# One fused attention-and-norm kernel: queries and keys projected transposed for two tiles at a time, and their 96-row stacks built by DMA through a DRAM scratch

## The chip, the cores and the metric

One core of one Trainium2 chip. The metric is the device time of one execution in microseconds (us); shorter is better.

## The reference, cut to what matters

```python
# x is (4, 1024, 256); 16 heads of 16; one tile of the kernel is 128 tokens
h = _layernorm(x) * (1 + ca) + sa            # sa, ca, ga, sb, cb, gb from silu(c) @ wmod, per batch
q, k, v = split(h @ qkv_w + qkv_b)
scores = q k^T / sqrt(16); scores = where((dist > 0) & (dist <= 128) & (k_gpos >= 0), scores, NEG)
local = softmax(scores) @ v                  # a window of 128 keys before each query
rq, (rk, rv) = h @ rq_w + rq_b, mean_of_16(h) @ rkv_w + rkv_b      # 64 pooled tokens, 4 heads
remote = (masked softmax(rq rk^T) @ rv) @ rout_w + rout_b
gate = sigmoid(local @ gl_w + remote @ gr_w)
x = x + ga * ((gate * local + (1 - gate) * remote) @ out_w + out_b)
h = _layernorm(x) * (1 + cb) + sb
x = x + gb * FFN(h)
return x
```

The kernel computes the last block as `x1 + gb * (layernorm(h) * ln_g + ln_b)` (`add_u`, `scale3`, `finish`).

## The kernel before, in words

The 4096 tokens are 32 tiles of 128; a batch has 8 of them. The five engines run one software pipeline written out by hand: in slot t each engine walks its own fixed list, and the letters say which tile each stage of the list works on. A (tile t+2): layer norm, transpose, modulation (`hT`) and the projection `project_qk`. K (tile t+1): values, the latent branch, and the stacks of queries and keys. S (tile t): window scores for the row maxima. T (tile t-1): transposed scores with exponents (`scores_t`, `exps`), masks (`mask`) and the product with the values (`sum_v`). C (tile t-2): gate, mix and output projection. D (tile t-3): second norm and last block. A loop of 8 slots is unrolled and run 4 times. Nothing but these lists and semaphores sets the order: every engine executes in order, so one waiting instruction holds back all behind it.

To keep float32 accuracy with bfloat16 matmuls, q and k are each split into three bfloat16 terms, and six products of them are summed by stacking: a head's 16 columns stand six times, in 96 rows. `project_qk` writes q and k of one tile (128 tokens by 512 columns) to `p_qkv`; `copy_qk` on DVE adds the bias into `qkf`; `part1` and `part2` on ACT write the first and second term, in all the places in which they stand, into `qtok` and `ktok`; `res1` and `part3` on POOL make the remainders and the third term. `stack(t, u)` on PE then transposes 8 heads at a time (u = 0 to 3: queries, keys, queries, keys) into `p_x`, and `stack_copy` on ACT copies them to `qst` (queries) and `kst` (keys).

The score matmuls of `scores` read the stacks for the row maxima (`maxima` on DVE writes `mtok`). `max_t` transposes the maxima, `copy_shift` and `shift` on DVE write them under the queries as 16 more rows, of which `kst` selects one per head (`pick`, a row pattern written once at the start), so that `scores_t` computes score minus maximum, and `exps` on ACT follows. POOL zeroes what lies outside of the window (`mask(m, g)`, four groups of four heads), and `sum_v(m, g)` on PE waits for `masked[g]`. On ACT `gate_tanh(c)` stands between `exps(m, 4)` and `exps(m, 5)` and waits for POOL's `difference(c)`, which waits for DVE's `local_out(c)`. SP only stores finished tiles inside the loop. At the start SP loads the inputs, sends the rows that DVE's `modulation_rows` makes through DRAM (`mod_rows`) to all partitions, and then queues the load of the last 24 tiles of x.

## Time and profile before

| | |
|---|---|
| median of 3 runs | 657.01 us (656.66 to 661.27) |
| the profiled execution | 658.29 us, its span 656.5 us |
| mean granted TensorE clock | 0.974 |
| PE busy | 566.5 us (86%) |
| DVE busy | 503.8 us (77%) |
| ACT busy | 484.9 us (74%) |
| POOL busy | 417.7 us (64%) |
| moved by DMA | 17.48 MB, mean 27 GB/s |

The span runs from the first to the last instruction; the device time holds 1.8 us more. PE's busy time counts matmuls that overlap, so the distance between the starts of two neighbours says more than their durations. The DMA engines are idle after the first 60 us but for one store per tile.

### The profile page before, as it was taken

To read this page: it belongs to the slowest core of one execution; us is meant where nothing else is said; L and a number is where in the kernel's file an instruction comes from. 1 tells how busy PE (TensorE), PEld (TensorE's weight loads), DVE (VectorE), ACT (ScalarE), POOL (GpSimd) and SP (SyncE) were. 2 spreads that over 40 slices of the span, in tenths; PEclk is the share of its full clock that TensorE was granted. 3 is DMA by queue.
4 is the path that set the end of the run, shared out by engine and by line. 5 is a ranking of instruction groups with operands and counts; after the bars stand their busy time and mean duration, and the time that the engine had idled before them with its cause. 6 is when DMAs were issued, how large, how long until landed. Compare 5 with 4: busy or idle time off the path is not lost. (4 is left out here: it accounts for less than half of the span.)

```text
span 656.5 us, 22130 instructions
## 1 busy us (share of the span) xinstructions
PE 566.5 (86%) x7535; PEld 415.4 (63%) x7535; DVE 503.8 (77%) x1390; ACT 484.9 (74%) x1066; POOL 417.7 (64%) x616
## 2 busy tenths in 40 slices
PE   2739999999979999999979999999979999999972
PEld 2237666776657666667756666766756666666651
DVE  5637888888868787888868788888868888888864
ACT  1687787778868787777768788777767778877760
POOL 3335566667756577766657576776656576677673
PEclk9879999999999999999989999999989999999986
DMA  8183000000000000000000000000000000000000
GB/s 262 63 292 96 2 2 2 11 10 10 11 15 9 10 10 7 6 10 10 10 15 10 9 10 11 10 2 10 10 15 10 9 10 11 10 6 6 11 18 16
DMA packets 13761, 17.48 MB, mean 27 GB/s; under 512 B 2980, under 2 KB 11836, under 8 KB 13628
## 3 DMA queue, kind: packets, MB, share of 16 engines
q1 hardware_dynamic: 10764, 14.52, 6.4%
q10 hardware_dynamic: 2864, 1.31, 0.8%
q8 instruction: 68, 1.11, 0.7%
q14 instruction: 65, 0.53, 0.3%
HBM read 11.61 MB, written 4.22 MB: 24 GB/s over the span
## 5 line engine op out<-in xcount | busy, mean ns | idle before, releaser
L554 ACT ACTIVATE pr<-p_y 128x512 f32<-128x512 f32 x232 | 135.0, 597 | 30.4 <-PE p_y L802 26.6
L1171 DVE TENSOR_REDUCE mtok<-p_x 128x3 bf16<-128x480 f32 (+3 forms) x192 | 113.5, 591 | 53.3 <-issue 29.6
L399 POOL TENSOR_SCALAR_AFFINE_SELECT pr<-pr 128x512 f32<-128x512 f32 x132 | 88.5, 670 | 49.7 <-ACT pr L554 46.0
L801 PE MATMUL p_y<-qst,kst 112*128 112x128 bf16 x464 | 71.3, 220 | 27.5 <-ACT pr L554 26.7
L403 POOL TENSOR_SCALAR_AFFINE_SELECT pr<-pr 128x512 f32<-128x512 f32 x116 | 89.7, 773 | 0.0
L802 PE MATMUL p_y<-qst,kst 112*128 112x128 bf16 x528 | 77.9, 219 | 3.1 <-ACT pr L556 3.1
L409 POOL TENSOR_TENSOR rstd<-ve,half 128x1 f32<-128x1 f32 x104 | 63.7, 620 | 26.5 <-DVE ve L1094 24.7
L427 POOL TENSOR_TENSOR dif<-local,rem 128x272 f32<-128x272 f32 x34 | 25.9, 762 | 85.0 <-DVE local L1224 85.0
L705 PE MATMUL p_qkv<-wqk,hT 128*128 128x512 f32 x136 | 69.1, 632 | 2.1 <-issue 1.2
L801 PEld LDWEIGHTS p_y<-qst,kst 112*128 112x128 bf16 x464 | 45.2, 101 | 40.4 <-issue 30.5
L545 ACT ACTIVATE qst<-p_x 96x1024 bf16<-96x1024 bf16 x66 | 67.3, 1019 | 2.5 <-PE p_x L748 0.5
L816 PE MATMUL p_pv<-pr,vp 128*18 128x128 f32 x1984 | 67.5, 275 | 1.2 <-POOL pr L403 1.2
L545 ACT ACTIVATE kst<-p_x 96x1024 bf16<-96x1024 bf16 x66 | 67.3, 1019 | 0.0
L778 PE MATMUL p_x<-kst,qst 96*32 96x160 bf16 x1792 | 61.9, 236 | 0.0
L816 PEld LDWEIGHTS p_pv<-pr,vp 128*18 128x18 f32 x1984 | 48.8, 98 | 18.1 <-issue 16.6
L594 ACT ACTIVATE th<-dif 128x16 f32<-128x16 f32 x34 | 7.8, 229 | 70.7 <-POOL dif L427 70.7
L802 PEld LDWEIGHTS p_y<-qst,kst 112*128 112x128 bf16 x528 | 50.1, 98 | 13.7 <-issue 4.2
L383 POOL TENSOR_TENSOR res<-qkf,qtok 128x256 f32<-128x256 f32 x34 | 23.3, 685 | 55.8 <-ACT ktok L532 55.8
L778 PEld LDWEIGHTS p_x<-kst,qst 96*32 96x32 bf16 x1792 | 28.1, 95 | 22.5 <-issue 10.3
L748 PE MATMUL p_x<-ident_bf,qtok 128*96 128x128 bf16 x528 | 40.3, 219 | 2.2 <-POOL ktok L391 1.4
L715 PE MATMUL p_qkv<-wv,hT 128*128 128x272 f32 x132 | 41.4, 439 | 0.0
L748 PE MATMUL p_x<-ident_bf,ktok 128*96 128x128 bf16 x528 | 40.3, 219 | 0.3 <-ACT kst L545 0.3
(159 smaller groups left out, 1498.6 us busy)
## 6 DMA issues: line engine op xcount, KB each, us to landing
out_y<-y SPq DMA_DIRECT2D x32, 128.0 KB, 2.4
x_all<-in_x SPq DMA_DIRECT2D x1, 3072.0 KB, 17.9
pr<-in_wmod SPq DMA_DIRECT2D x1, 1024.0 KB, 10.1
row<-in_rows SPq DMA_DIRECT2D x1, 816.0 KB, 7.0
x_all<-in_x SPq DMA_DIRECT2D x1, 768.0 KB, 4.9
wqk<-in_qkv_w ACTq DMA_DIRECT2D x1, 512.0 KB, 3.8
pr<-in_wmod SPq DMA_DIRECT2D x1, 512.0 KB, 5.3
pr<-mod_rows SPq DMA_DIRECT2D x1, 512.0 KB, 4.0
```

The source lines that it names most:

```text
L399: ins = pool.affine_select(out=own, in_=own, compare_op=ALU.is_ge, fill=0.0, base=-1, pattern=[[0, 4], [1, P]], channel_multiplier=-1)
L403: ins = pool.affine_select(out=prev, in_=prev, compare_op=ALU.is_ge, fill=0.0, base=-1, pattern=[[0, 4], [-P, P]], channel_multiplier=P + 1)
L409: pool.tensor_tensor(rstd_[:, :], ve_[:, :], half[:, :], ALU.pow).then_inc(s_rstd, 1)
L545: act.activation(dst, p_x[u % 2][0:KS, :].bitcast(BF16).rearrange("p (h n) -> p h n", h=8), ACT.Copy)\
L554: act.activation(pr[:, 2 * i:2 * i + 2, :, :], src, ACT.Exp).then_inc(exp_done[i], 1)
L705: ins = pe.matmul(p_qkv[:, :], hT[:, t[1] % 2, k, :], wqk[:, k, :], start=(k == 0), stop=(k == KC - 1))
L748: ins = pe.transpose(dst[:, j * P:(j + 1) * P], src[:, 8 * (u // 2) + j, :], ident_bf[:, :])
L778: ins = pe.matmul(win[g * QG:(g + 1) * QG, h - h0, :], qst[0:KS, t[1] % RING, h, g * QG:(g + 1) * QG], keys[:, at:at + WIN], start=False, ...
L801: pe.matmul(p_y[i % 2][:, at:at + P], kst[0:KS + H, h, (n - 1) % NB, :], q, start=True, stop=True)
L802: ins = pe.matmul(p_y[i % 2][:, at + P:at + 2 * P], kst[0:KS + H, h, n % NB, :], q, start=True, stop=True)
L816: ins = pe.matmul(p_pv[32 * j:32 * j + VC, g * P:(g + 1) * P], vp[:, (n - 1 + a) % RING, h, :], pr[:, h, a, :], start=(a == 0 or n % NB == ...
L1171: dve.tensor_reduce(mtok[:, KS + h0:KS + h1], p_x[i % 2][:, 0:(h1 - h0) * w].rearrange("p (h n) -> p h n", n=w), AX_X, ALU.max, negate=Tru ...
```

## The change

Queries and keys are projected transposed: `project_half` computes, for a pair of tiles (256 tokens as the moving columns), the queries in one slot and the keys in the next, so that features lie on the partitions. The pipeline is longer: A works on tile t+4, the projection (P) on t+3, the split into terms (Q) on t+2. The three terms are written once each into `terms`. `stack`, `stack_copy`, `qtok`, `ktok` and `pick` are gone. Instead SP stores the three terms of a half to a DRAM scratch (`store_terms`, 128 partitions by 6 runs of 512 bytes) and reads the stack back with six transfers (`load_stack`, each 16 partitions by 16 runs of 512 bytes). Queries are handled in even slots, keys in odd ones. The shift is one row under the queries, moved by SP from `mrow` (`shift`), with a constant row of ones under the keys. The edge mask of a score group is written by four matmuls on column quarters instead of one. The start of the program runs four shortened slots.

```diff
--- before.py
+++ after.py
-Q_SLOTS = {1: (2, 5, 1), 2: (1, 6, 4), 3: (0, 1, 1)}
-K_SLOTS = {1: (0, 3, 1), 2: (3, 6, 2), 3: (4, 5, 1)}
-
+Q_TERMS = (0, 0, 0, 1, 1, 2)
+K_TERMS = (0, 1, 2, 0, 1, 0)
...
+            def shift(t):
+
+                wait_apart(sp, (mrow_ready, done(t)), (st_psum[NP - 1], done(back(t, 4))))
+                sp.dma_start(q_of(t)[KS:KS + 1, :, :], mrow[:, :]).then_inc(shift_loaded[t[1] % 2], 16)
+
+            def store_terms(r):
+
+                half = r[1] % 2
+                wait_apart(sp, (part3_ready, done(r)), (stack_loaded[half], halves(back(r, 2), 16 * NTERM)))
+                sp.dma_start(scr[half].rearrange("t p n -> p t n"), terms[:, half, :, :, :].rearrange("p s b n -> p (s b) n"))\
+                  .then_inc(terms_stored[half], 16)
+
+            def load_stack(r):
+
+                half = r[1] % 2
+                pair = pair_of(r)
+                wait_apart(sp, (terms_stored[half], halves(r, 16)), (st_psum[NP - 1], done(back(r, 7 if half else 3))))
+                n = pair[1] % NB
+                for i in range(NTERM):
+                    if half:
+                        dst = kst[i * HD:(i + 1) * HD, :, n:n + 2, :].rearrange("d h r n -> d h (r n)")
+                    else:
+                        dst = qst[i * HD:(i + 1) * HD, n // 2 % 2, :, :]
+                    s0 = (K_TERMS if half else Q_TERMS)[i] * KC
+                    sp.dma_start(dst, scr[half][s0:s0 + KC].rearrange("b (h d) n -> d (b h) n", d=HD))\
+                      .then_inc(stack_loaded[half], 16)
...
+            def slot(t, stages):
+                r, m, d = back(t, -2), back(t, 1), back(t, 3)
+                Q, T, D_ = ("Q" in stages, "T" in stages, "D" in stages)
+                if T:
+                    shift(m)
+                if Q:
+                    store_terms(r)
+                if Q and t[1] % 2:
+                    load_stack(r)
+                if D_:
+                    store(d)
+                if Q and t[1] % 2 == 0:
+                    load_stack(r)
+
+            slot((0, -2), "Q")
+            slot((0, -1), "Q")
...
             def res1(t):
 
                 pool.wait_ge(part1_ready, done(t))
-                pool.tensor_tensor(heads(res[:, 0:D]), heads(qkf[:, 0:D]), slots(qtok, Q_SLOTS[1])[:, :, 0, :], ALU.subtract)
-                pool.tensor_tensor(heads(res[:, D:2 * D]), heads(qkf[:, D:2 * D]), slots(ktok, K_SLOTS[1])[:, :, 0, :],
-                                   ALU.subtract).then_inc(res_ready, 1)
+                half = t[1] % 2
+                pool.tensor_tensor(qkf[:, half, :, :], qkf[:, half, :, :], terms[:, half, 0, :, :], ALU.subtract)\
+                    .then_inc(res_ready, 1)
 
             def part3(t):
+
                 pool.wait_ge(part2_ready, done(t))
-                pool.tensor_tensor(slots(qtok, Q_SLOTS[3])[:, :, 0, :], heads(res[:, 0:D]),
-                                   slots(qtok, Q_SLOTS[2])[:, :, 0, :], ALU.subtract)
-                pool.tensor_tensor(slots(ktok, K_SLOTS[3])[:, :, 0, :], heads(res[:, D:2 * D]),
-                                   slots(ktok, K_SLOTS[2])[:, :, 0, :], ALU.subtract).then_inc(part3_ready, 1)
+                half = t[1] % 2
+                pool.tensor_tensor(terms[:, half, 2, :, :], qkf[:, half, :, :], terms[:, half, 1, :, :], ALU.subtract)\
+                    .then_inc(part3_ready, 1)
...
             def part1(t):
 
+                half = t[1] % 2
                 act.wait_ge(qk_copied, done(t))
-                act.wait_ge(stack_psum[3], done(back(t, 1)))
-                act.activation(slots(qtok, Q_SLOTS[1]), rep(qkf[:, 0:D], Q_SLOTS[1]), ACT.Copy)
-                act.activation(slots(ktok, K_SLOTS[1]), rep(qkf[:, D:2 * D], K_SLOTS[1]), ACT.Copy).then_inc(part1_ready, 1)
+                act.wait_ge(terms_stored[half], halves(back(t, 2), 16))
+                act.activation(terms[:, half, 0, :, :], qkf[:, half, :, :], ACT.Copy).then_inc(part1_ready, 1)
 
             def part2(t):
+
+                half = t[1] % 2
                 act.wait_ge(res_ready, done(t))
-                act.activation(slots(qtok, Q_SLOTS[2]), rep(res[:, 0:D], Q_SLOTS[2]), ACT.Copy)
-                act.activation(slots(ktok, K_SLOTS[2]), rep(res[:, D:2 * D], K_SLOTS[2]), ACT.Copy).then_inc(part2_ready, 1)
-
-            def stack_copy(t, u):
-
-                act.wait_ge(stack_psum[u], done(t))
-                act.wait_ge(st_psum[NP - 1], done(back(t, 3)))
-                hs = slice(8 * (u // 2), 8 * (u // 2) + 8)
-                dst = kst[0:KS, hs, t[1] % NB, :] if u % 2 else qst[0:KS, t[1] % RING, hs, :]
-                act.activation(dst, p_x[u % 2][0:KS, :].bitcast(BF16).rearrange("p (h n) -> p h n", h=8), ACT.Copy)\
-                   .then_inc(stack_copied[u], 1)
+                act.activation(terms[:, half, 1, :, :], qkf[:, half, :, :], ACT.Copy).then_inc(part2_ready, 1)
...
-                a, k, m, c = back(t, -2), back(t, -1), back(t, 1), back(t, 2)
-                A, K, S, T, C = ("A" in stages, "K" in stages, "S" in stages, "T" in stages, "C" in stages)
+                a, r, m, c = back(t, -LEAD), back(t, -2), back(t, 1), back(t, 2)
+                A, Q, S, T, C = ("A" in stages, "Q" in stages, "S" in stages, "T" in stages, "C" in stages)
+                if Q:
+                    part1(r)
                 if C:
                     out_t(c)
                 if T:
                     lat_oT(m)
-                if K:
-                    part2(k)
-                if T:
                     exps(m, 0)
+                if Q:
+                    part2(r)
+                if T:
                     exps(m, 1)
                 if S:
                     lat_exp(t)
...
                     exps(m, 5)
                     remote(m)
                     exps(m, 6)
-                if K:
-                    stack_copy(k, 0)
-                    stack_copy(k, 1)
-                if T:
                     exps(m, 7)
+                if S:
+                    lat_pT(t)
                 if C:
                     mixed_t(c)
-                if K:
-                    stack_copy(k, 2)
-                if A:
-                    part1(a)
-                if S:
-                    lat_pT(t)
-                if K:
-                    stack_copy(k, 3)
 
...
-            def project_qk(t):
-                pe.wait_ge(hT_ready, done(t))
-
-                pe.wait_ge(rem_ready, done(back(t, 3)))
-                if t[1] < 2 and isinstance(t[0], int):
-                    pe.wait_ge(v_copied, done(back(t, 1)))
-                for k in range(KC):
-                    ins = pe.matmul(p_qkv[:, :], hT[:, t[1] % 2, k, :], wqk[:, k, :], start=(k == 0), stop=(k == KC - 1))
+            def project_half(t):
+
+                pair, half = pair_of(t), t[1] % 2
+                pe.wait_ge(hT_ready, done(back(pair, -1)))
+
+                pe.wait_ge(rem_ready, done(back(t, 4)))
+                pe.wait_ge(v_copied, done(back(t, 2)))
+                pe.wait_ge(qk_copied, done(back(t, 1)))
+                r = pair[1] % 4
+                for b in range(KC):
+                    for k in range(KC):
+                        ins = pe.matmul(p_qkv[:, 2 * b * P:2 * (b + 1) * P], wqk[:, k, half * D + b * P:half * D + (b + 1) * P],
+                                        hT[:, r:r + 2, k, :], start=(k == 0), stop=(k == KC - 1))
                 ins.then_inc(qk_psum, 1)
...
-            def stack(t, u):
...
-                src = (qtok, ktok)[u % 2]
-                dst = p_x[u % 2][0:KS, :].bitcast(BF16)
-                for j in range(8):
-                    ins = pe.transpose(dst[:, j * P:(j + 1) * P], src[:, 8 * (u // 2) + j, :], ident_bf[:, :])
-                ins.then_inc(stack_psum[u], 1)
...
-                if i == 0:
-                    pe.wait_ge(stack_copied[0], done(t))
-                    pe.wait_ge(stack_copied[1], done(t))
-                    pe.wait_ge(stack_copied[2], done(t))
-                elif i == 1:
-                    pe.wait_ge(stack_copied[3], done(t))
-                else:
-                    pe.wait_ge(s_max[i - 2], done(t))
+                if i == 0 and t[1] % 2 == 0:
+                    for half in range(2):
+                        pe.wait_ge(stack_loaded[half], halves(back(t, -half), 16 * NTERM))
+                pe.wait_ge(s_max[(i - 2) % NS], done(t if i >= 2 else back(t, 1)))
...
-                    pe.matmul(ends, ident_bf[:, :], edge[:, :].unsqueeze(1).to_broadcast([P, h1 - h0, 2 * QG]).rearrange("p h (e n) -> p h e n", n=QG),
-                              start=True, stop=True)
+                    for g in range(4):
+                        pe.matmul(ends[g * QG:(g + 1) * QG], ident_bf[:, g * QG:(g + 1) * QG],
+                                  edge[:, :].unsqueeze(1).to_broadcast([P, h1 - h0, 2 * QG]).rearrange("p h (e n) -> p h e n", n=QG),
+                                  start=True, stop=True, tile_position=(0, g * QG))
...
-                pe.transpose(p_qkv[:, 0:P // 2].bitcast(BF16), mtok[:, :], ident_bf[:, :]).then_inc(mT_psum, 1)
+                pe.transpose(p_qkv[0:H, 0:P // 2].bitcast(BF16), mtok[:, :], ident_bf[:, :]).then_inc(mT_psum, 1)
...
-                pe.wait_ge(shift_ready, done(t))
+                pe.wait_ge(shift_loaded[t[1] % 2], halves(t, 16))
...
-                if K:
-                    stack(k, 0)
                 if T:
                     scores_t(m, 7)
-                if K:
-                    stack(k, 1)
-                if A:
-                    project_qk(a)
+                if PR:
+                    project_half(h)
                 if C:
                     mixed_t(c)
-                if K:
-                    stack(k, 2)
                 if S:
                     lat_p_t(t)
-                if K:
-                    stack(k, 3)
                 if C:
                     project_out(c)
...
             def copy_qk(t):
 
+                half = t[1] % 2
                 dve.wait_ge(qk_psum, done(t))
-                dve.wait_ge(part3_ready, done(back(t, 1)))
-                dve.tensor_tensor(qkf[:, :], p_qkv[:, :], row[:, R_QK:R_QK + 2 * D], ALU.add).then_inc(qk_copied, 1)
+                dve.wait_ge(part3_ready, done(back(t, 2)))
+                dve.tensor_tensor(qkf[:, half, :, :], p_qkv[:, :].rearrange("p (b n) -> p b n", b=KC),
+                                  bc(bqk[:, half, :], 2 * P), ALU.add).then_inc(qk_copied, 1)
...
             def copy_shift(t):
+
                 dve.wait_ge(mT_psum, done(t))
-                dve.tensor_copy(mrow[KS:KS + H, :], p_qkv[KS:KS + H, 0:P // 2].bitcast(BF16)).then_inc(mrow_ready, 1)
-
-            def shift(t):
-
-                dve.wait_ge(mrow_ready, done(t))
-                dve.tensor_copy(qst[KS:KS + H, t[1] % RING, :, :],
-                                mrow[KS:KS + H, :].unsqueeze(1).to_broadcast([H, H, P])).then_inc(shift_ready, 1)
+                dve.wait_ge(shift_loaded[(t[1] - 1) % 2], halves(back(t, 1), 16))
+                dve.tensor_copy(mrow[:, :], p_qkv[0:H, 0:P // 2].bitcast(BF16)).then_inc(mrow_ready, 1)
...
             dve.wait_ge(loaded_x0, 16)
-            b0, b1 = (0, 0), (0, 1)
-            bn1(b0)
-            moments1(b0)
-            add_eps1(b0)
-            norm1(b0)
+            dve.wait_ge(su_act, SA_QK)
+            slot((0, -4), "A")
+            slot((0, -3), "AP")
             weights()
-            copy_qk(b0)
-            bn1(b1)
-            moments1(b1)
-            add_eps1(b1)
-            copy_v(b0)
-            norm1(b1)
-            pool_tokens(b0)
-            pool_twice(b0)
+            dve.wait_ge(loaded_x1, 16)
+            slot((0, -2), "APQ")
             modulation_rows()
-            copy_qk(b1)
             dve.wait_ge(loaded_bd, 16)
-            copy_rk(b0)
-            copy_rq(b0)
-            copy_rv(b0)
-            spread_rv(b0)
+            slot((0, -1), "APQK")
...
```

On POOL, in a slot of the loop (mask 0 is the pair of AFFINE_SELECT, `xb` is `add_bias`, `dif` is `difference`), before:

```order
L290 ISA
L399 AFFINE_SELECT pr<-pr 128x4x128
L403 AFFINE_SELECT pr<-pr 128x4x128
L389 TENSOR_TENSOR qtok<-res,qtok 128x16x16
L391 TENSOR_TENSOR ktok<-res,ktok 128x16x16
L423 REGISTER_ALU
L427 TENSOR_TENSOR dif<-local,rem 128x272
```

and now:

```order
L458 TENSOR_TENSOR rstd<-ve,half 128x1
L440 TENSOR_TENSOR terms<-qkf,terms 128x512
L291 ISA
L448 AFFINE_SELECT pr<-pr 128x4x128
L452 AFFINE_SELECT pr<-pr 128x4x128
L485 ISA
L485 TENSOR_TENSOR xb<-x_all,obg 128x256
L472 REGISTER_ALU
L476 TENSOR_TENSOR dif<-local,rem 128x272
```

The third term (`part3`) has moved from behind mask 0 to ahead of it, as one instruction of 512 elements, and `add_bias` from the slot's start to behind mask 0.

On PE, the last third of a slot (L705 is `project_qk`, L748 `stack`, L872 `mixed_t`, L836 `lat_p_t`, L880 `project_out`, L816 `sum_v` of groups 1 to 3), before:

```order
L748 MATMUL p_x<-ident_bf,ktok 96x128 x8
L705 MATMUL p_qkv<-wqk,hT 128x512 x2
L872 MATMUL p_misc<-cst,mix 128x128 x2
L748 MATMUL p_x<-ident_bf,qtok 96x128 x8
L836 MATMUL p_a<-cst,lp 128x128 x2
L748 MATMUL p_x<-ident_bf,ktok 96x128 x8
L880 ISA
L880 MATMUL p_misc<-wo,mixT 128x256
L880 ISA
L880 MATMUL p_misc<-wo,mixT 128x256
L816 MATMUL p_pv<-pr,vp 18x128 x24
```

and now:

```order
L723 MATMUL p_qkv<-hT,wqk 128x256 x4
L871 MATMUL p_misc<-cst,mix 128x128 x2
L835 MATMUL p_a<-cst,lp 128x128 x2
L879 ISA
L879 MATMUL p_misc<-wo,mixT 128x256
L879 ISA
L879 MATMUL p_misc<-wo,mixT 128x256
L814 MATMUL p_pv<-pr,vp 18x128 x24
```

`mixed_t`, `lat_p_t` and `project_out` now follow each other with nothing between them.

On SP, the loop's beginning, before:

```order
L349 UNCONDITIONAL_BRANCH
L349 ISA
L343 ISA
L343 DMA out_y<-y 128x256
L342 REGISTER_ALU
```

and now (slots 0 and the beginning of slot 1):

```order
L397 UNCONDITIONAL_BRANCH
L397 ISA
L350 DMA qst<-mrow 1x16x128
L291 ISA
L356 DMA scr_q<-terms 128x6x256
L291 ISA
L376 ISA
L376 DMA out_y<-y 128x256
L291 ISA
L371 DMA qst<-scr_q 16x16x256 x6
L291 ISA
L350 DMA qst<-mrow 1x16x128
```

In an even slot the six loads of the query stack stand behind the store of y and ahead of the next slot's shift row. (In an odd slot the key loads stand ahead of the store of y.)

## Rows read from the trace of the kernel before

**Rows 1.** Waits of PE over the whole execution: us in total, times, longest us.

```profile
PE p_y L801 <- ACT pr L554: 26.7, 30, 1.0
```

**Rows 2.** PE's timeline over one slot: start us, us busy; idle time in brackets.

```profile
299.50 0.23 PE L790 MATMUL p_qkv<-ident_bf,mtok 128*128 128x128 bf16 x1
...
302.56 0.22 PE L801 MATMUL p_y<-qst,kst 112*128 112x128 bf16 x1
...
306.24 0.63 PE L816 MATMUL p_pv<-pr,vp 128*18 128x128 f32 x16
306.81 0.23 PE L772 MATMUL p_x<-edge,ident_bf 128*128 128x128 bf16 x1
...
311.13 0.22 PE L801 MATMUL p_y<-qst,kst 112*128 112x128 bf16 x1 [0.88 <-ACT pr L554]
...
311.35 0.61 PE L748 MATMUL p_x<-ident_bf,ktok 128*96 128x128 bf16 x8
311.80 1.94 PE L705 MATMUL p_qkv<-wqk,hT 128*128 128x512 f32 x4
313.57 0.38 PE L872 MATMUL p_misc<-cst,mix 128*128 128x128 f32 x2
...
314.91 1.08 PE L880 MATMUL p_misc<-wo,mixT 128*128 x4
315.92 1.51 PE L816 MATMUL p_pv<-pr,vp 128*18 128x128 f32 x48
317.36 0.23 PE L790 MATMUL p_qkv<-ident_bf,mtok 128*128 128x128 bf16 x1
```

**Rows 3.** ACT's timeline over the same slot.

```profile
302.98 1.33 ACT L554 ACTIVATE pr<-p_y 128x512 f32<-128x512 f32 x2 [0.43 <-PE p_y L802]
...
310.41 0.58 ACT L554 ACTIVATE pr<-p_y 128x512 f32<-128x512 f32 x1
...
316.83 0.36 ACT L576 ACTIVATE lpT<-p_a 128x256 f32<-128x256 f32 x1
```

**Rows 4.** POOL's timeline over the same slot.

```profile
305.04 0.64 POOL L403 TENSOR_SCALAR_AFFINE_SELECT pr<-pr 128x512 f32<-128x512 f32 x1
...
309.48 0.77 POOL L427 TENSOR_TENSOR dif<-local,rem 128x272 f32<-128x272 f32 x1 [2.50 <-DVE local L1224]
```

**Rows 5.** POOL's groups by form: busy us, mean ns of one, idle before.

```profile
L280 POOL TENSOR_TENSOR wo<-rem,pr 128x512 f32<-128x512 f32 x2 | 2.5, 1265 | 0.0
```

**Rows 6.** DVE's timeline over the same slot.

```profile
299.80 0.23 DVE L1176 COPY mrow<-p_qkv 16x128 bf16<-16x128 bf16 x1
...
314.38 0.72 DVE L1272 SCALAR_TENSOR_TENSOR y<-h,rstd,ux 128x256 f32<-128x256 f32 x1
```

**Rows 7.** DMA view: a queue (packets, MB, share), then issues (KB, us to landing).

```profile
q10 hardware_dynamic: 2864, 1.31, 0.8%
...
x_all<-in_x SPq DMA_DIRECT2D x1, 3072.0 KB, 17.9
...
b<-mod_rows SPq DMA_DIRECT2D x1, 512.0 KB, 8.5
```

**Rows 8.** SP's timeline at the start of the program.

```profile
32.44 0.32 SPq L332 DMA_DIRECT2D mod_rows<-qst  x1
34.56 0.35 SPq L334 DMA_DIRECT2D pr<-mod_rows  x1
...
37.17 0.59 SPq L336 DMA_DIRECT2D b<-mod_rows  x1
37.81 0.45 SPq L338 DMA_DIRECT2D x_all<-in_x  x1
```

**Rows 9.** All engines' timeline at the start of the program.

```profile
17.05 3.75 PE L705 MATMUL p_qkv<-wqk,hT 128*128 128x512 f32 x4 [1.16 <-issue]
...
27.20 0.73 DVE L1052 TENSOR_SCALAR qst<-p_y 4x256 f32<-4x256 f32 x2
...
47.07 0.29 PE L790 MATMUL p_qkv<-ident_bf,mtok 128*128 128x128 bf16 x1 [9.36 <-ACT kst L516]
```

More of the change, by code:

```diff
@@ L69, with build @@
 R_END = R_GR + HD
-def build(nc, x, qkv_w, rq_w, rq_b, rkv_w, rk_b, rout_w, rout_b, out_w, c_t, wmod, rows, consts, out):
+def build(nc, x, qk_b, ones, qkv_w, rq_w, rq_b, rkv_w, rk_b, rout_w, rout_b, out_w, c_t, wmod, rows, consts, out):
     ctx = ExitStack()
@@ L461, in slot @@
                     mask(m, 1)
-                    mask(m, 2)
                 if D:
@@ L1412, in constants @@
         c[LD + q, C_IND + q * CH:C_IND + (q + 1) * CH] = 1
-    for h in range(H):
-        c[KS + h, C_SEL + h] = 1
     c[CH:, C_VAL] = 1
```

222 lines of the change are left out of this document (100 added, 122 removed).

## The prediction

> **What bounds the kernel now.** I read PE's timeline first. A slot runs from one `max_t` (L790) to the next, 299.50 to 317.36, 17.86 us [rows 2], and the starts stand close behind each other: PE works nearly all the time. What ends its few waits is told by its list of waits: `scores_t` waits for exponents in 30 of the slots, 26.7 us together [rows 1]; the row at 311.13 is one such place [rows 2]. The reader is to see why it waits there, since this is a chain through all engines that removing PE work doesn't shorten. I count T from the slot's start, 299.50. `scores(t, 5)` begins at T 7.31 (306.81); DVE then takes its maxima, scales the second norm and makes `local`; POOL subtracts at T 9.98 (309.48) [rows 4], 2.67 behind; ACT's tanh lets `exps(m, 5)` start at T 10.91 [rows 3], and the last `scores_t` starts at T 11.63 [rows 2]. From `scores(t, 5)` to there are 4.32 us, whatever PE does meanwhile. So PE work bounds most of the slot and this chain one part of it, and a cut of PE work counts only where no such chain takes over.
>
> **Part 1, what PE loses.** Four groups of stack transposes go: one takes 0.45 from start to start (311.35 to 311.80) [rows 2], together 1.8 us a slot. One stands just ahead of the wait at 311.13, so without it that wait grows by the same 0.45. The projection keeps its 1.77 us (311.80 to 313.57) [rows 2]: eight passes of 256 columns for four of 512. An edge matmul takes 0.16 with its weights (306.81; the wider ones somewhat more); in four quarters it costs between 0.1 and 0.3. I take 0.1, as the score matmuls in quarters also overlap, and so 0.06 gained six times. If all of this arrived, a slot would take 17.86 - 1.8 - 0.36 = 15.7 us.
>
> **Part 2, what ACT and DVE lose.** Stack copies and the spreading of terms leave ACT, and the shift copy leaves DVE. Neither bounds a slot (74% and 77% busy), so I give them nothing but shorter queues.
>
> **Part 3, the third term moves ahead of mask 0.** This is the term that I trust most. Before, mask 0 was done at T 6.18 (305.04 + 0.64) [rows 4] and `sum_v(m, 0)` began at T 6.74 [rows 2], without a wait. Now ACT runs `exps(m, 0)` at T 3.48 [rows 3], then `part2` to about T 4.7, and POOL must do `part3` before mask 0. As one POOL instruction on 512 elements it has a near row: 1.265 us [rows 5]. It ends at T 6.0, mask 0 is a pair of 0.6 and 0.64 and ends at T 7.3, and `sum_v(m, 0)`, which PE would now reach at T 6.5, starts there. `scores(t, 5)` follows 0.57 behind as before, at T 7.9, and with the unchanged 4.32 the last `scores_t` starts at T 12.2 instead of 11.63.
>
> **Part 4, the tail of the slot.** From there 0.22 + 1.77 + 0.22 bring PE to `lat_p_t` at T 14.4. ACT now copies `lpT` ahead of `mixT`: two copies of 256 columns, 0.36 each [rows 3]. The transposes take 0.38 to be there [rows 2], so `mixT` is there at about T 15.5 and `project_out` starts at T 15.6, against T 15.41 before; two stacks used to fill this time. Then 1.01 for `project_out` (314.91 to 315.92) and 1.44 for `sum_v` (to 317.36) [rows 2]: the slot ends at T 18.1. So all of PE's saving turns into waits, and a slot without any DMA trouble costs +0.2. Bounds: -0.5, if `part3` runs at twice that row's speed, to +0.6.
>
> **Part 5, the shift row.** `mrow` is there at T 0.53 (299.80 + 0.23) [rows 6]. The nearest row for a small transfer and its wait is that of the modulation rows: issued at 32.44, the next one at 34.56, 2.1 us [rows 8]. In an odd-to-even step SP is free, the row lands at T 2.8, and `scores_t(m, 0)` wanted it at T 3.06 (302.56) [rows 2]: no cost. In an even-to-odd step it is different. SP is in order, and ahead of the shift it waits for y, which is done at T 15.6 (314.38 + 0.72) [rows 6], then issues the store and six loads, each 0.4 to 0.5 us to issue [rows 8]. The shift's packets also stand behind those of the loads: 6 x 256 = 1536 runs of 512 bytes. No row shows such loads. Below is the mean packet of the ACT queue: 0.8% of 16 x 656.5 us over 2864 packets [rows 7] is 29 ns on one engine, 1.8 ns with 16, so the loads would be bound by their issue, 2.9 us. Above is the load of x: 3072 rows of 1 KB in 17.9 less 2.1 fixed, 5.1 ns a row, 7.9 us. Less what stood ahead of it (the last broadcast landed 8.5 behind 37.17, at 45.7, and x at 37.81 + 17.9 = 55.7 [rows 7, 8]) it is 3.3 ns, 5.0 us. I take this, as it is the same queue and direction, and a row of half the size is hardly half the price. Then the loads land at T 16.1 + 2.1 + 5.0 = 23.2, the shift just behind at T 5.3 of the odd slot, 2.3 us late (0.4 and 5.2 at the ends). Behind the waiting `scores_t` stands everything that PE has left in the slot, and ACT's `exps(m, 0)`, POOL's `part3` and mask 0 behind it: the slot grows by all of it.
>
> **Part 6, the keys in an odd slot.** `part3` ends at T 6.0 + 2.3 = 8.3. The store takes 2.1 + 768 x 3.3 ns = 4.6, the loads 7.1: T 20.1 with SP's own steps. The slot ends at T 20.4. Nothing is lost, but with a margin of a few tenths; at 5.1 ns the keys come 3.9 us late as well.
>
> **Part 7, the start.** PE began slot 0 at 47.07 [rows 9]. The new start hides less: DVE needs tile 0 and 1 through transposes and modulation and then a projection at the low clock (3.75 us against 1.94 in the loop; the clock was at 1.2 GHz there) [rows 2, 9] before it makes the weights, and the same again with tile 2 before `modulation_rows`, which stood at 27.20 [rows 9]. I put this at 11 us (5 to 14): two such waits of some 6 us. SP then issues the load of x at 48.8 instead of 37.81 and it lands 17.9 later, at 66.7 [rows 7, 8]. All transfers for the stacks are issued behind it on the same queue: query terms to 69.2, query loads to 76.3 with the key store behind them to 78.8, key loads 7.1 more, 86. That is +39 us (27 with the lower price and the smaller delay).
>
> **The sum.** 657.0 + 39 + 32 x 0.2 + 16 x 2.3 = 739; I say **740 us**, slower. The profiled execution was 658.29 with a span of 656.5, so the new one should show a span near 739. A change within 1% can't be told from none here.
>
> **A rule that speaks against the change.** The loads write 16 partitions each. If the rate depends on how many partitions a transfer spans, six of them in a row are slow one after the other. The Trainium skill, page "SBUF — State Buffer", section on the DMA port swizzle, says just this: four neighbouring partitions share a port, 16 ports at 27.2 GB/s. By that page 16 partitions reach four ports, and the six loads, 786 KB, would take about 7.2 us, an estimate; no row here shows a transfer on so few partitions. This is a rival.
>
> **Rivals.** (1) The loads are slow, 7.9 us by the undeducted x row: the shift is 5.2 late, the keys 3.9, 16 x 9.1 = 146 and the start 4 more: 845; with something between this and my price, 790. For it speaks the narrow destination, against it the 29 ns packets of the ACT queue. Chance 0.27. (2) The loads are cheap, 1.8 ns: 657 + 30 + 6 + 6 = 699, chance 0.18. (3) The other side: the chain of part 3 isn't there, because PE's list doesn't really wait for mask 0 (`part3` much shorter than the row of 512), and the shift comes in time. Slots of 15.7 give -2.16 x 32 = -69, the start +39: 627. It decides at 1.2 us a slot, since the start must be won back first. The idle 0.56 ahead of `sum_v` is all the room that the trace shows, so 0.05. (4) Long waits lower PE's clock again in the loop, as at the start: each low stretch doubles matmul time, and 760 to 800 comes out even with quick loads; 0.08. My own case, 720 to 760, has 0.42.
>
> **The range** takes in the cheap loads and most of the slow ones: 695 to 820. Slower by over 1%: 0.94; faster by over 1%: 0.05; within: 0.01.
>
> **What would show it.** Right: PE's `scores_t` of group 0 waits for a DMA in every second slot, some 2 us; `sum_v(m, 0)` waits for POOL in nearly all; `project_out` waits for ACT by 0.9; slots alternate, about 18 and 20 us; slot 0 begins at 80 to 90 us with SP's first store of terms behind x. Wrong: `scores(t, 0)` of even slots waiting for the key stack (rival 1); even slots under 17 us; the first stacks there before 60 us, if transfers of one queue overtake each other.

## The result

| | before | changed |
|---|---|---|
| median | 657.55 us (656.66 to 661.27) | 803.75 us (800.23 to 806.76) |
| profiled span | 656.5 us | 799.6 us |
| mean granted TensorE clock | 0.974 | 0.857 |

The ratio is 1.2208, with a 95% interval of 1.2142 to 1.2274. The changed kernel is 146 us slower. That lies in the range of 695 to 820, but outside my own likeliest case, 720 to 760, and 64 us above the forecast of 740.

### The profile page after: what moved, and what is told of

Read it like the earlier page. It is cut to its first block, busy times and chain, and to the rows that moved or that the text cites. A ratio compares the mean times of both kernels' runs of the same rounds, so it can differ in the third digit from the quotient of the medians.

```text
span 799.6 us, 21397 instructions
## 1 busy us (share of the span) xinstructions
PE 569.0 (71%) x7131; PEld 429.9 (54%) x7131; DVE 473.4 (59%) x1366; ACT 304.9 (38%) x864; POOL 385.9 (48%) x552
## 3 DMA queue, kind: packets, MB, share of 16 engines
q1 hardware_dynamic: 94110, 54.55, 36.4%
## 4 chain that ended last, share of the span: by engine, by line
issue 38%; PE 21%; POOL 21%; DVE 6%; DMA 6%; ACT 4%; SPq 2%; POOLq 1%; DVEq 0%; ACTq 0%
PE p_qkv L723 9%; PE p_misc L879 5%; POOL rstd L458 4%; POOL qkf L433 4%; POOL dif L476 3%; POOL xb L485 3%; POOL pr L452 2%; POOL pr L448 2%; DMA scr_q<-terms 2%; ACT pr L589 2%; POOL terms L440 2%; ACT mixT L634 2%; SPq L371 2%; DMA qst<-mrow 1%; PE p_misc L871 1%
## 5 line engine op out<-in xcount | busy, mean ns | idle before, releaser
L799 PE MATMUL p_y<-qst,kst 97*128 97x128 bf16 x464 | 80.1, 239 | 91.1 <-DMA qst<-mrow 53.3
L799 PEld LDWEIGHTS p_y<-qst,kst 97*128 97x128 bf16 x464 | 49.1, 109 | 113.4 <-DMA qst<-mrow 60.3
L440 POOL TENSOR_TENSOR terms<-qkf,terms 128x512 bf16<-128x512 f32 x34 | 39.3, 1157 | 136.2 <-ACT terms L581 136.2
L800 PE MATMUL p_y<-qst,kst 97*128 97x128 bf16 x528 | 89.7, 243 | 15.5 <-DMA qst<-mrow 13.0
L723 PE MATMUL p_qkv<-hT,wqk 128*128 128x256 f32 x280 | 85.1, 458 | 0.9 <-ACT hT L565 0.9
L814 PE MATMUL p_pv<-pr,vp 128*18 128x128 f32 x1984 | 69.5, 280 | 3.2 <-POOL pr L452 2.5
L800 PEld LDWEIGHTS p_y<-qst,kst 97*128 97x128 bf16 x528 | 55.4, 109 | 27.9 <-DMA qst<-mrow 14.3
L723 PEld LDWEIGHTS p_qkv<-hT,wqk 128*128 128x128 f32 x280 | 61.0, 229 | 11.4 <-ACT hT L565 1.3
L814 PEld LDWEIGHTS p_pv<-pr,vp 128*18 128x18 f32 x1984 | 49.1, 99 | 22.8 <-issue 14.6
L879 PE MATMUL p_misc<-wo,mixT 128*128 (+1 forms) x136 | 38.6, 407 | 29.0 <-ACT mixT L634 29.0
L597 ACT ACTIVATE oT<-p_pv 128x512 f32<-128x512 f32 x34 | 20.3, 597 | 74.3 <-PE p_pv L814 67.3
L769 PE MATMUL p_x<-edge,ident_bf 128*32 128x192 bf16 (+1 forms) x672 | 47.4, 264 | 0.0
L879 PEld LDWEIGHTS p_misc<-wo,mixT 128*128 128x128 f32 x136 | 23.5, 193 | 38.9 <-ACT mixT L634 27.4
L490 POOL TENSOR_TENSOR ux<-x,b 128x256 f32<-128x256 f32 x35 | 26.0, 742 | 37.4 <-DVE x L1230 24.6
```

Of the source, the lines that this page charges most:

```text
L440: pool.tensor_tensor(terms[:, half, 2, :, :], qkf[:, half, :, :], terms[:, half, 1, :, :], ALU.subtract)\
L723: ins = pe.matmul(p_qkv[:, 2 * b * P:2 * (b + 1) * P], wqk[:, k, half * D + b * P:half * D + (b + 1) * P], hT[:, r:r + 2, k, :], start=(k ...
L799: pe.matmul(p_y[i % 2][:, at:at + P], kst[0:KS + 1, h, (n - 1) % NB, :], q, start=True, stop=True)
L800: ins = pe.matmul(p_y[i % 2][:, at + P:at + 2 * P], kst[0:KS + 1, h, n % NB, :], q, start=True, stop=True)
L814: ins = pe.matmul(p_pv[32 * j:32 * j + VC, g * P:(g + 1) * P], vp[:, (n - 1 + a) % RING, h, :], pr[:, h, a, :], start=(a == 0 or n % NB == ...
L879: ins = pe.matmul(p_misc[:, 0:D], mixT[:, k * P:(k + 1) * P], wo[:, bass.ds(batch(t) * (KC * D // NB) + k * D, D)], start=(k == 0), stop=( ...
```

## The profile after

The page of the changed kernel: busy times, the granted clock, and the busiest DMA queue.

```profile
PE 569.0 (71%) x7131; PEld 429.9 (54%) x7131; DVE 473.4 (59%) x1366; ACT 304.9 (38%) x864; POOL 385.9 (48%) x552
...
PEclk9755799998988898989989688989889597979896
...
q1 hardware_dynamic: 94110, 54.55, 36.4%
```

PE issues fewer matmuls and is busy for as long as before: the stacks' work went, and a lower clock took its place. ACT fell from 74% to 38% busy, and none of that shows as a gain in the time.

The waits of PE (us in total, times, longest us); all are in the loop but the wait for `kst`, which is in the start:

```profile
PE p_y L799 <- DMA qst<-mrow: 53.3, 17, 5.5
PE p_y L799 <- ACT pr L589: 37.9, 30, 1.5
PE p_misc L879 <- ACT mixT L634: 29.0, 34, 1.0
PE p_x L761 <- DMA kst<-scr_k: 26.5, 1, 26.5
...
PE p_y L800 <- DMA qst<-mrow: 13.0, 3, 4.4
```

The wait for exponents was 26.7 [rows 1]. The waits for the shift row (53.3 + 13.0 = 66.3 us, since L799 and L800 are both `scores_t`) and for `mixT` are new. PE's timeline through an even slot (L788 is `max_t`, L799 `scores_t`, L814 `sum_v`, L769 an edge mask, L723 `project_half`, L879 `project_out`) and the odd slot behind it:

```profile
329.78 0.22 PE L788 MATMUL p_qkv<-ident_bf,mtok 128*16 128x128 bf16 x1
...
332.72 0.22 PE L799 MATMUL p_y<-qst,kst 97*128 97x128 bf16 x1
...
336.78 0.63 PE L814 MATMUL p_pv<-pr,vp 128*18 128x128 f32 x16
337.23 0.24 PE L769 MATMUL p_x<-edge,ident_bf 128*32 128x128 bf16 x4
...
341.44 0.22 PE L799 MATMUL p_y<-qst,kst 97*128 97x128 bf16 x1 [1.33 <-ACT pr L589]
...
341.68 1.96 PE L723 MATMUL p_qkv<-hT,wqk 128*128 128x256 f32 x8
...
344.92 1.10 PE L879 MATMUL p_misc<-wo,mixT 128*128 x4 [0.84 <-ACT mixT L634]
...
347.28 0.22 PE L788 MATMUL p_qkv<-ident_bf,mtok 128*16 128x128 bf16 x1
...
355.89 0.29 PE L799 MATMUL p_y<-qst,kst 97*128 97x128 bf16 x1 [5.51 <-DMA qst<-mrow]
...
362.36 0.94 PE L814 MATMUL p_pv<-pr,vp 128*18 128x128 f32 x16
...
373.17 0.22 PE L788 MATMUL p_qkv<-ident_bf,mtok 128*16 128x128 bf16 x1
```

The even slot takes 17.50 us, against 17.86 before [rows 2]. The odd one takes 25.89. It is among the three odd slots with the longest wait for the row, 5.1 to 5.5 us; eleven others wait 4.0 to 4.4, slot 3 waits 1.1 and slot 1 not at all. Its `scores_t` starts at T 8.61 instead of T 2.94, 5.67 later, and everything stands behind it. From there to `sum_v` it takes 6.47 instead of 4.06. The windows of just these two stretches, odd and even (us, busy times, then the granted clock, DMA share and GB/s), say why:

```profile
355.89:362.36 6.47, 6.47 (x69) 4.24 (x69) 2.73 (x6) 3.98 (x13) 3.03 (x4) 0.50 0.19 62
```

```profile
332.72:336.78 4.06, 3.83 (x69) 2.57 (x67) 3.16 (x8) 3.63 (x13) 2.44 (x4) 1.00 0.06 19
```

After the 5.51 us without a matmul, PE works at 0.50, the level of 1.2 GHz, for the same 69 matmuls. SP's timeline shows where the row stood: the load of the queries is issued at 346.02 and the row (L350) at 348.99, and it was used at 355.89.

```profile
346.02 2.78 SPq L371 DMA_DIRECT2D qst<-scr_q  x6
348.99 0.52 SPq L350 DMA_DIRECT2D qst<-mrow  x1
...
361.73 2.78 SPq L371 DMA_DIRECT2D kst<-scr_k  x6
```

The start, on the same engine: the long load of x, then the first store of terms, whose issue alone is held for 10.67 us, and the loads behind it.

```profile
48.04 0.45 SPq L344 DMA_DIRECT2D x_all<-in_x  x1
48.62 10.67 SPq L356 DMA_DIRECT2D scr_q<-terms  x1
66.42 2.78 SPq L371 DMA_DIRECT2D qst<-scr_q  x6
...
75.43 2.76 SPq L371 DMA_DIRECT2D kst<-scr_k  x6
```

**Where the time went**, from the starts of `max_t`. The table counts slot 0 as part of the start, since the changed kernel enters it and then waits in it for the keys until 83.19.

| | before | changed | difference |
|---|---|---|---|
| up to slot 1 | 66.99 | 104.02 | +37.0 |
| slots 1 to 31 | 560.7 | 666.4 | +105.8 |
| behind the last | 28.9 | 29.2 | +0.3 |

The 16 odd slots rose from 18.17 to 24.37 on average, +99. Of this, some 63 us are waits for the row, and 29 are the stretch from `scores_t` to `sum_v`, as run 3 shows. The 15 even ones cost 6 us more together: seven take 17.50, the others 18.3 to 20.3. Five of these (slots 8, 16, 18, 24 and 28) have the low clock in a part of the slot, three (2, 10 and 26) don't.

## The experiments

Medians; in brackets the kernel before on the same chip; "loop" is slots 1 to 31 in the profile (before: 560.7, changed: 666.4), read from one execution of each. The changed kernel itself was not timed again on these chips, so a run's ratio is to be held against its 1.2208.

**Run 1, the row on another queue.** Everything else as in the changed kernel.

```diff
-                if T:
-                    shift(m)            # SP
+                if T:
+                    shift(m)            # ACT, ahead of lat_oT, act.dma_start(...)
```

> The changed kernel, but the shift row is issued by ACT (between out_t and lat_oT), so it travels on ACT's DMA queue and not behind the six query loads on SP's. Theory Q (the row is late only because it stands behind the loads on one queue): the 17 long waits of scores_t for the row (53.3 us) fall under 1 us each, odd slots go from about 25 to about 18 us, and the loss in low clock behind the waits goes as well. The key stack, hidden so far in the long odd slots, then comes about 1 us late in even slots. Total 690 us (680 to 710). Rival E (the 16 DMA engines are simply busy with the loads, whatever the queue): the row stays 5 us late and the total stays within 10 us of 804.

776.98 us [659.99], 1.1768 (1.1717 to 1.1819), loop 642.3. SP's loads, ACT's issue of the row, and PE's `scores_t` behind it:

```profile
347.10 3.42 SPq L366 DMA_DIRECT2D qst<-scr_q  x6
349.44 0.51 ACTq L579 DMA_DIRECT2D qst<-mrow  x1
```

```profile
355.29 0.23 PE L798 MATMUL p_y<-qst,kst 97*128 97x128 bf16 x1 [3.32 <-DMA qst<-mrow]
```

Nothing stands ahead of the row on its own queue, and still PE has it only 5.85 us after its issue, 8.19 after that of the loads. I had expected 690 if order were all, and within 10 us of 804 if the loads held the row back on any queue. The result is nearer to the second: a queue of its own doesn't get the row past the loads' data. Whether the two share the DMA engines or the way into SBUF is not told apart.

**Run 2, the same bytes to spread partitions.** The copies of a head's 16 features are interleaved in the stack, so that a load still writes 16 partitions, but every sixth one and not neighbours. The products and their sum are the same.

```diff
-dst = kst[i * HD:(i + 1) * HD, :, n:n + 2, :]
+dst = kst[i:KS:NTERM, :, n:n + 2, :]
-dst = qst[i * HD:(i + 1) * HD, n // 2 % 2, :, :]
+dst = qst[i:KS:NTERM, n // 2 % 2, :, :]
```

> The changed kernel, but row i of a feature's six terms stands at partition 6d+i instead of 16i+d, for queries and keys alike: the same six loads of 256 runs of 512 bytes, each now spread over 96 partitions instead of 16 neighbouring ones. Theory N (the loads are slow because a transfer writes 16 neighbouring partitions): they become bound by their issue, 2.8 us, instead of the 7.6 us that the trace shows (first issue at 346.02, the row behind them there at 355.8, less 2.1 fixed). The row is then at most 1 us late, and the total is about 685 to 700 us. Rival P (the price is 4.9 ns for each run of 512 bytes, wherever it goes): nothing changes, 800 to 808.

759.23 us [659.99], 1.1499 (1.1445 to 1.1554), loop 629.0. The DMA view (count, KB, median us from issue to landing) of the changed kernel, then of this one:

```profile
qst<-scr_q SPq DMA_DIRECT2D x102, 128.0 KB, 4.5
```

```profile
qst<-scr_q SPq DMA_DIRECT2D x102, 128.0 KB, 2.7
```

The same 54.55 MB take 23.3% of the engines' time instead of 36.4%. So the neighbouring destinations were what made a run dear. The time stayed well above the 685 to 700 that I expected, because the row still stands behind six issues, and their issue is now longer (SP, and the `scores_t` that ends the wait):

```profile
333.04 3.87 SPq L371 DMA_DIRECT2D qst<-scr_q  x6
337.10 0.56 SPq L350 DMA_DIRECT2D qst<-mrow  x1
```

```profile
340.31 0.29 PE L799 MATMUL p_y<-qst,kst 97*128 97x128 bf16 x1 [2.90 <-DMA qst<-mrow]
```

**Run 3, PE kept busy through the wait.** 24 matmuls of 512 columns, added work whose result is overwritten, ahead of the wait in odd slots.

```diff
+                pe.wait_ge(exp_done[(i - 2) % NP], done(t if i >= 2 else back(t, 1)))
+                if i == 0 and t[1] % 2 == 0:
+                    for _ in range(24):
+                        pe.matmul(p_y[0][:, :], ident_bf[:, :], <smask0, 512 columns>, start=True, stop=True)
                 pe.wait_ge(shift_loaded[t[1] % 2], halves(t, 16))
-                pe.wait_ge(exp_done[(i - 2) % NP], done(t if i >= 2 else back(t, 1)))
```

> The changed kernel with extra work that the result doesn't need: in odd slots PE runs 24 bfloat16 matmuls of 512 columns, about 5.2 us, into p_y ahead of scores_t(m, 0), while the shift row is on its way. Theory C (after 5.5 us without work PE's clock stands at 1.2 GHz for some 7 us, and this costs 2.4 us in each odd slot on top of the wait): the granted clock goes back to about 0.95 and the total falls by 16 x 2.4 = 38, to 765. Rival (the 2.4 us are the chain through ACT and POOL, not the clock): the clock rises and the total stays at 804 or grows by a few us where the wait is shorter than the extra work.

792.63 us [659.99], 1.2006 (1.1971 to 1.2041), loop 655.4. The added matmuls, the first score matmul, and the windows of the stretches before and behind it:

```profile
357.04 5.34 PE L795 MATMUL p_y<-smask,ident_bf 128*128 128x512 bf16 x24
362.22 0.22 PE L803 MATMUL p_y<-qst,kst 97*128 97x128 bf16 x1
```

```profile
361.00:366.30 5.30, 5.06 (x78) 3.10 (x76) 2.65 (x6) 3.65 (x13) 2.46 (x4) 1.00 0.07 20
...
370.80:376.00 5.20, 4.31 (x17) 3.44 (x17) 3.27 (x12) 2.13 (x6) 3.70 (x6) 0.67 0.79 89
```

`scores_t` to `sum_v` takes 4.07 again (362.22 to 366.29), so the idle time does lower the clock and costs 2.4 us there. Summed over the 16 odd slots, this stretch gives back 28.8 us. But the 24 matmuls last 5.2 us: with them `scores_t` starts at T 8.12 in every odd slot, where it started at T 7.1 to 7.5 in eleven of them and at T 2.9 and 4.2 in slots 1 and 3. That costs 17.6 us. The difference is the 11 us by which the loop got shorter, where I had expected 38. In this slot the clock falls later as well, at 370.86, where PE had waited 1.24 us for exponents; that happens in some slots of the changed kernel too, and run 8 shows that it hangs on this wait.

**Run 4, `mixT` first.** `mixed_t` on ACT ahead of `lat_pT`.

```diff
+                if C:
+                    mixed_t(c)
                 if S:
                     lat_pT(t)
-                if C:
-                    mixed_t(c)
```

> The changed kernel, but ACT copies mixT ahead of lpT at the end of a slot. My step on the tail (project_out waits for mixT behind lpT, 0.84 to 1.0 us in each of 34 slots, 29.0 us in all, and this sets the slot's end): 804 - 33 x 0.8 = 777. Rival (mask 3 on POOL or the DVE's list sets the slot's end, so the wait only moves to sum_v): within 5 us of 804.

789.81 us [659.99], 1.1991 (1.1919 to 1.2064), loop 652.1. PE's wait for `mixT` falls from 0.84 to 0.35 in a slot, and a clean even slot (one without a low clock or a wait for the row) from 17.50 to 17.02. That is over half of the 0.8 that I had expected, and the median is 12.8 above the expected 777:

```profile
326.96 1.10 PE L879 MATMUL p_misc<-wo,mixT 128*128 x4 [0.35 <-ACT mixT L634]
```

**Run 5, x on ACT's queue.** The load of the last 24 tiles of x is issued by ACT behind its second short slot of the start.

```diff
-            sp.dma_start(x_all[:, (XPAD + NB) * D: ...], x[NB:NT] ...).then_inc(loaded_x, 16)
...
             slot((0, -3), "AP")
+            act.dma_start(x_all[:, (XPAD + NB) * D: ...], x[NB:NT] ...).then_inc(loaded_x, 16)
```

> The changed kernel, but the load of the last 24 tiles of x is issued on ACT's queue early in the start (after the second shortened slot), not on SP's queue ahead of the first store of terms. Theory S (the first stacks are late because their transfers stand behind 3 MB of x on one queue): that store, whose issue took 10.67 us from 48.62 and which was there at 66.4, is there at about 52 (the five broadcasts remain ahead), slot 0 scores start at 66 to 70 instead of 83.2, and the total falls by 14 to 17 us from about 806 on this chip, to 790. Rival (the late modulation rows, 42.75 against 32.44, and the six loads themselves set the start): within 5 us of 806.

796.10 us [658.83], 1.2069 (1.2003 to 1.2134). The start's wait for keys falls from 26.5 to 18.0 us, and slot 1 begins at 94.2 instead of 104.0: 10 us, where I had expected 14 to 17. The loop is at 668.7, about as it was.

```profile
PE p_x L761 <- DMA kst<-scr_k: 18.0, 1, 18.0
```

**Runs 6 to 8, edits together.** Run 6 is runs 1 and 2. Run 7 adds runs 4 and 5. Run 8 also puts ACT's `gate_tanh(c)` behind `exps(m, 5)`.

> Both of e1 and e2: the shift row on ACT's queue and the six terms of a feature spread over 96 partitions. Each alone left the row 2 to 4 us late, on its own queue because the 16 engines were still busy with the slow loads, with quick loads because it stood behind them on the queue. If these two are the whole of it, the row now costs at most 0.5 us, no slot sees the low clock, the keys land at T 14.5, and odd slots come down to the 17.5 us of even ones: 683 to 692. Rival: something else makes odd slots long (SP's order, the keys), and they stay above 19: over 705.

> e6 with the mixT copy ahead of the lpT copy on ACT (e4) and the x load on ACT's queue (e5). If the effects add: 687 less 15 (0.48 us a slot, as e4 measured) less 14 to 17, so 655 to 660, level with the kernel before. All four are repairs of the change's own costs.

> e7 with ACT's gate_tanh behind exps(m, 5) instead of ahead of it. The chain scores(t, 5), maxima, second norm, local, POOL difference, tanh, exps(m, 5), last scores_t made PE wait 1.33 us in each slot with the change (0.88 to 1.0 before). If this chain is what kept PE's saving from showing, the wait goes and slots fall by up to 1.3 us: 657 less up to 40, so 617 to 635. Rival: mask 3 on POOL, or the mix for mixed_t, is late instead and takes most of it: above 645.

| | median | ratio (95%) | loop |
|---|---|---|---|
| run 6 | 708.22 [658.83] | 1.0759 (1.0705 to 1.0813) | 573.8 |
| run 7 | 685.81 [658.83] | 1.0354 (1.0303 to 1.0405) | - |
| run 8 | 671.98 [658.83] | 1.0174 (1.0127 to 1.0220) | 549.6 |

The profiled execution of run 7 took 695.28 us, well above its median, so its loop is not compared. All three runs missed what I had expected of them, 683 to 692, 655 to 660 and 617 to 635.

Runs 1 and 2 alone gave 24 and 37 us in the loop, together 93: with both, the row lands 2.2 us after its issue (median) and the sum of its waits is 6.2 us. That run 6 is still 16 us above the range is for the greater part the clock at another place. In seven slots `project_half`, behind PE's wait for exponents, takes 3.3 to 3.7 us instead of 1.97, 10 us together, as here in slot 13:

```profile
330.83 0.22 PE L798 MATMUL p_y<-qst,kst 97*128 97x128 bf16 x1 [1.32 <-ACT pr L587]
...
331.22 3.41 PE L722 MATMUL p_qkv<-hT,wqk 128*128 128x256 f32 x8
```

The granted clock over 331.10 to 334.50 is 0.57. In run 8 the wait for exponents is gone, and `project_half` takes 1.97 in all 32 slots. So the low clock at this place came with that wait, though the same wait is not followed by it in most slots, and what decides that I can't say. Even slots of run 8 stay at 17.02. A new wait of 0.86 us stands ahead of `project_half`:

```profile
PE p_qkv L723 <- issue: 29.4, 32, 1.1
```

```profile
349.68 0.23 ACT L625 ACTIVATE th<-dif 128x16 f32<-128x16 f32 x1 [1.52 <-POOL dif L467]
349.81 0.38 ACT L618 ACTIVATE rem<-p_qkv 128x272 f32<-128x272 f32 x1
```

```profile
350.29 1.96 PE L723 MATMUL p_qkv<-hT,wqk 128*128 128x256 f32 x8 [0.86 <-issue]
```

The profile names "issue", but the code tells which wait it is: `project_half` writes the bank from which ACT's `remote` (L618) copies, and `remote` stood behind `gate_tanh` (L625) and its wait for POOL.

**Runs 9 to 11, on the kernel before.** Run 9 has the quarters of the edge masks alone, run 10 has `gate_tanh` behind `exps(m, 6)`, run 11 has both.

```diff
-                    pe.matmul(ends, ident_bf[:, :], <edge>, start=True, stop=True)
+                    for g in range(4):
+                        pe.matmul(ends[g * QG:(g + 1) * QG], ident_bf[:, g * QG:(g + 1) * QG], <edge>,
+                                  start=True, stop=True, tile_position=(0, g * QG))
```

```diff
-                if C:
-                    gate_tanh(c)
                 if T:
                     exps(m, 5)
                     remote(m)
                     exps(m, 6)
+                if C:
+                    gate_tanh(c)
```

> The kernel before with one part of the change alone: the edge mask of a score group is written by four matmuls on column quarters instead of one. In the trace of the changed kernel four quarters take 0.08 to 0.09 us from start to start, where one whole matmul took 0.16 to 0.18. Six of them in a slot: 4 x 0.09 + 2 x 0.08 = 0.5 us less PE work. Theory (PE bounds the slot and the chain from scores(t, 5) moves forward with it, since five of the six edges stand ahead of it): 33 slots x 0.5 = 16 us less, 640 to 645 against 657 to 660. Rival (the gain turns into waits, as the saving of the stacks did in the changed kernel): within 4 us of the kernel before.

> The kernel before, with ACT's gate_tanh moved from behind exps(m, 4) to behind exps(m, 6): exps(m, 5), remote and exps(m, 6) no longer stand behind the wait for POOL's difference. Nothing of the change is in it. PE waited 26.7 us for these exponents in 30 slots. Theory: the wait was ACT's order alone and nothing else is late there; 0.88 us in most slots comes back, 630 to 638. Rival (as in the experiment with five edits on the changed kernel: a wait for the remote copy, for the mixture or for a mask comes up within 0.3 us of it): 645 to 655.

> The kernel before with both: quarters for the edge masks, and gate_tanh behind exps(m, 6). Queries and keys stay as before, in SBUF by PE and ACT. If the two gains add: 0.5 + 0.88 us a slot, 612 to 622. If the chains behind (mixture, masks, norm statistics) take over: 630 to 640. Either is below both kernels.

| | median [before 659.89] | ratio (95%) | clean slot | loop |
|---|---|---|---|---|
| run 9 | 655.05 | 0.9938 (0.9912 to 0.9963) | 17.64 | 556.2 |
| run 10 | 629.47 | 0.9534 (0.9496 to 0.9573) | 16.83 | 531.9 |
| run 11 | **622.58** | 0.9425 (0.9393 to 0.9457) | 16.60 | 524.0 |

Run 9's gain is 4.8 us, a third of the 16 that I had expected. The kernel before, from the matmul ahead of an edge to the first score matmul behind it, and then around the edge behind `sum_v`; and run 9 at the same places:

```profile
300.60 0.61 PE L845 MATMUL p_misc<-lpT,bvd 128*128 128x128 f32 x4
301.04 0.25 PE L772 MATMUL p_x<-edge,ident_bf 128*128 128x192 bf16 x1
301.22 0.39 PE L778 MATMUL p_x<-kst,qst 96*32 96x160 bf16 x12
...
306.24 0.63 PE L816 MATMUL p_pv<-pr,vp 128*18 128x128 f32 x16
306.81 0.23 PE L772 MATMUL p_x<-edge,ident_bf 128*128 128x128 bf16 x1
306.97 0.32 PE L778 MATMUL p_x<-kst,qst 96*32 96x160 bf16 x8
```

```profile
281.45 0.61 PE L847 MATMUL p_misc<-lpT,bvd 128*128 128x128 f32 x4
281.99 0.27 PE L773 MATMUL p_x<-edge,ident_bf 128*32 128x192 bf16 x4
282.08 0.38 PE L780 MATMUL p_x<-kst,qst 96*32 96x160 bf16 x12
...
287.10 0.63 PE L818 MATMUL p_pv<-pr,vp 128*18 128x128 f32 x16
287.55 0.24 PE L773 MATMUL p_x<-edge,ident_bf 128*32 128x128 bf16 x4
287.60 0.32 PE L780 MATMUL p_x<-kst,qst 96*32 96x160 bf16 x8
```

At the first place it is 0.62 and 0.63. The edge looks like 0.09 instead of 0.18, but it also starts 0.10 later: four quarters save nothing there, nor at four more of the six edges of a slot. Only the edge of `scores(t, 5)`, behind `sum_v`, gains: from `sum_v` to the first score matmul it is 0.50 instead of 0.73. The chain to the last exponents begins by so much earlier, and this 0.23 is all that a clean slot gains (17.86 to 17.64).

Run 10 takes away the wait for exponents [rows 1], and nothing takes its place: 1.03 us a slot, at the good end of the 630 to 638 that I had expected. In run 11 the two gains add.

**Run 12, the changed kernel at its best.** Run 8 with `gate_tanh` behind `exps(m, 6)`, and POOL's `rstd3_of` between masks 2 and 3.

> The changed kernel with the five edits of the last experiment and two changes of order: gate_tanh on ACT behind exps(m, 6) instead of behind exps(m, 5), so that the projection of PE no longer waits for the remote copy that stood behind gate_tanh (0.86 us in nearly all slots), and the third norm's square root on POOL between mask 2 and mask 3 instead of ahead of both, so that the last sum_v waits less for the masks (0.31). Theory: even slots go from 17.02 to 16.1 to 16.4 us, odd slots by as much less what the shift row takes: 645 to 655 against 672. Rival: odd slots stay because the six loads and the row set them, and the time falls by half of that, 660.

669.14 us [659.89], 1.0136 (1.0091 to 1.0180), loop 545.0. The time is above both my theory, 645 to 655, and its rival, 660. Clean even slots do reach 16.40. The odd ones stay at 16.6 to 18.2 in many places, and waits for the row add up to 23.7 us. The fair mate on the kernel before is run 11, which has the quarters and the same place for `gate_tanh` (loop 524.0). Against it the changed kernel still loses 21 us in the loop and, up to slot 1, 23 us (89.4 against 66.2). So no run shows the change ahead of the kernel before.

## Why the prediction was right and wrong

**The sign and the places** were right. PE waits for the shift row in every second slot, for `mixT` by 0.84 in the others, and at the start for stacks that stand behind x. That the saved PE time would turn into waits held too. The sum had +39 for the start and +43 for the loop; measured are +37 and +106.

**Part 5 was mis-sized: this is the main miss.** I took 3.3 ns a run of 512 bytes, arguing that half a row is hardly half the price. From the first load's issue to the row's use are 9.87 us in the slot shown (346.02 to 355.89), 8.4 to 9.9 over the odd slots from slot 5 on, and 9.0 on average. Less the 2.1 us fixed that is 6.3 to 7.8 us, 4.1 to 5.1 ns a run: the top of that part's range, up to its upper bound. The row is there at T 8.6 of the odd slot shown, and at T 7.5 on average, where I had T 5.3. In the slot shown 2.8 of this is the price and 0.6 that the slot before was shorter. Run 2 shows the cause, the 16 neighbouring partitions. The rate in the paragraph on the rule, 7.2 us for six loads, was the better estimate: the measured 6.3 to 7.8 lie around it. Here the trace agrees with the Trainium skill, page "SBUF — State Buffer", section on the DMA port swizzle. I had a rule that named the mechanism, and against it only the 29 ns of mixed packets on another queue, and gave it 0.27.

**The clock was left out of the sum.** Rival (4) stood there as a case of its own, but a long wait and a low clock come together: the longer wait of rival (1) brings 2.41 us more in the slot shown (6.47 against 4.06). The time is rivals (1) and (4) together. For that slot: 17.50 + 5.67 + 2.41 + 0.31 in the rest = 25.89; the average odd slot is 24.37. Run 3 gives back the 2.4 where it was lost, 28.8 us in all odd slots, and loses 17.6 of it again, since the added work is longer than most of the waits.

**Parts 1 to 4** said +0.2 for a clean slot; it is -0.36, inside the bounds of -0.5 to +0.6. `sum_v(m, 0)` began at T 7.00 (I had 7.3), since `part3` and mask 0 were a little quicker, and the last `scores_t` at T 11.66, not 12.2, which is where it stood before. The chain of part 3 is there: mask 0 ends at 336.73 in the slot shown, and `sum_v` starts at 336.78. But it made `sum_v` only 0.26 later than before, and PE's list shows hardly a wait for it (2.5 us in 6 slots), because PE itself came late: it had waited 0.18 for DVE's `xn` just ahead. And the quarters of the edge behind `sum_v` won back about as much. So the term that I trusted most cost next to nothing, partly by luck. The tail was as described: two copies ahead of `project_out`, a wait of 0.84, shown by run 4, which took 0.48 of it back. **The edges** were wrong in mechanism: not 0.06 gained six times, but nothing at five edges and 0.23 at the one behind `sum_v` (run 9).

**Part 6** was right for another reason: PE never waits for the keys in the loop, but because the odd slot is 5 us longer than I had it (loads issued at 361.73, wanted at 373.2). Rival (1)'s 3.9 us for the keys did not come, so its 845 was too high.

**Part 7** was right: +37.0 up to slot 1 against +39, and run 5 shows that x on the same queue was 10 us of it. Of the other 27, 9 are the longer setup (`max_t` of slot 0 at 56.4 instead of 47.07). I put the rest down to the chain of store, load, store, load, one behind the other; no run changes that chain.

**Rival (3)** asked whether slots could be as short as 15.7 us. Even run 12 doesn't get its clean slots below 16.38: the list of PE's waits then has DVE's `xn` and mixture, and POOL's masks.

## What to carry to other kernels

A transfer in a loop is priced by its destination as well. Look at where its partitions lie, and at what is queued behind it: 16 neighbouring ones were dear here, 16 spread over 96 were not. If a tiny transfer is needed soon, neither its own queue nor a faster bulk load is enough alone; here the two gave 24 and 37 us alone, and 93 together. Added work that keeps the clock up must not be longer than the wait that it fills. Before building a change that takes work from a busy engine, look at the longest repeated wait of the engine that bounds the kernel: here it was one line's place in ACT's list, worth 4.7% by itself, and more than anything that the change saved. And a matmul's distance to its follower must be read together with its distance from the one ahead, or a gain is seen that only moved.
